# Roots and gates of an attention pair in a PSUM work bank, and the pair's steps at other times in the common order

## The reference

```python
q = _rmsnorm(q, q_rms_w); k = _rmsnorm(k, k_rms_w)
omega_eff = jax.nn.softplus(omega) * slopes
gate = jax.nn.softplus(jnp.einsum('bthd,hd->bht', k, u_n) / math.sqrt(D))
bias = -dist * omega_eff * gate
attn = jax.nn.softmax(q @ k.T / math.sqrt(D) + bias)        # causal
x = _layernorm(x + attn @ v @ Wproj)
h = silu(x @ w1) * (x @ w2); h = gelu(h @ h1); h = gelu(h @ h2)
x = _layernorm(x + h @ w3)
```

## Time and profile before

| | |
|---|---|
| median of 3 runs | 3588.65 us (3587.58 to 3588.75) |
| profiled execution | 3589.89 us, span 3588.1 us |
| granted TensorE clock, mean | 0.959 |
| TensorE, VectorE, ScalarE, GpSimd busy | 90%, 51%, 50%, 42% of the span |
| pairs | 16, each 143 to 144 us |

### The profile page before, as it was taken

How to read it: one execution, slowest core, us unless ns; L and a number is a source line. 1 busy time by engine, 2 the same in 40 slices (tenths; PEclk the granted TensorE clock), 3 DMA queues, 4 the chain that set the end, 5 groups by cost and what they waited for, 6 DMA issues and landing times. The chain is left out here.

```text
span 3588.1 us, 45839 instructions
## 1 busy us (share of the span) xinstructions
PE 3216.2 (90%) x15472; PEld 2476.9 (69%) x15472; DVE 1842.8 (51%) x3921; ACT 1789.9 (50%) x3057; POOL 1513.0 (42%) x1318
## 2 busy tenths in 40 slices
PE   3989989889889898898998988958999999899999
PEld 3756757667567676675665766747877777688887
DVE  7576576665765766657656566614222222133222
ACT  1656656666666666666665666733222232232222
POOL 4565566566655665566655655631111110000000
PEclk8999999999999999999999999979999999999999
DMA  2231322322313223123132231343222331222120
GB/s 71 70 88 25 83 57 54 88 53 59 89 40 91 56 54 88 47 62 91 24 86 56 55 88 36 75 117 97 88 89 85 96 88 65 84 88 71 36 71 18
DMA packets 196538, 249.12 MB, mean 69 GB/s; under 512 B 67280, under 2 KB 95056, under 8 KB 196176
## 3 DMA queue, kind: packets, MB, share of 16 engines
q1 hardware_dynamic: 196304, 246.19, 26.2%
HBM read 84.86 MB, written 43.52 MB: 36 GB/s over the span
## 5 line engine op out<-in xcount | busy, mean ns | idle before, releaser
L366 POOL TENSOR_TENSOR e_lo<-e_all,e_hi 128x512 fp32r<-128x512 f32 (+1 forms) x832 | 1043.9, 1260 | 855.6 <-ACT e_all L606 721.8
L606 ACT ACTIVATE e_all<-ps_s,bias 128x512 f32<-128x512 f32 (+3 forms) x1280 | 781.0, 621 | 213.9 <-PE ps_s L901 143.5
L599 ACT ACTIVATE e_hi<-ps_s,bias 128x512 fp32r<-128x512 f32 (+1 forms) x832 | 558.4, 671 | 300.8 <-PE ps_s L899 178.2
L786 DVE TENSOR_REDUCE maxes<-ps_m 128x1 f32<-128x512 f32 x768 | 520.6, 687 | 356.5 <-PE ps_m L879 347.7
L879 PE MATMUL ps_m<-k_ext,q_max 128*128 128x512 f32 (+3 forms) x1280 | 477.8, 390 | 122.7 <-DVE maxes L786 74.3
L898 PE MATMUL ps_s<-q_twice,k_split 128*128 128x512 f32 (+3 forms) x1280 | 481.0, 376 | 0.7
L899 PE MATMUL ps_s<-q_ext,k_ext 128*128 128x512 f32 (+3 forms) x1280 | 475.7, 372 | 0.0
L932 PE MATMUL ps_v<-e_lo,v_main 128*66 128x512 f32 (+1 forms) x832 | 442.5, 532 | 14.9 <-POOL e_lo L366 14.9
L879 PEld LDWEIGHTS ps_m<-k_ext,q_max 128*128 128x128 f32 x1280 | 244.2, 192 | 302.6 <-DVE maxes L786 138.7
L783 DVE CUSTOM_DVE_ANT_0 ps_m<-ps_m,mask_row 128x128 f32<-128x128 f32 (+3 forms) x512 | 253.0, 497 | 287.2 <-PE ps_m L879 285.4
L916 PE MATMUL ps_v<-e_all,v_full 128*66 128x512 f32 (+2 forms) x896 | 333.3, 454 | 0.0
(11 more groups left out here) (212 smaller groups left out, 6137.8 us busy)
## 6 DMA issues: line engine op xcount, KB each, us to landing
q_twice<-q_max SPq DMA_DIRECT2D x256, 128.0 KB, 2.3
yt<-y_out SPq DMA_DIRECT2D x128, 130.0 KB
k_ext<-kq_hi SPq DMA_DIRECT2D x128, 128.0 KB, 2.3
q_max<-kq_hi SPq DMA_DIRECT2D x128, 128.0 KB, 2.4
k_split<-kq_hi SPq DMA_DIRECT2D x128, 128.0 KB, 2.4
k_split<-kq_lo SPq DMA_DIRECT2D x128, 128.0 KB, 2.4
q_ext<-kq_lo SPq DMA_DIRECT2D x128, 128.0 KB, 2.4
y_in<-yt SPq DMA_DIRECT2D x128, 128.0 KB, 3.1
```

What stands on the lines that cost most here:

```text
L366: on.tensor_tensor(e_lo[:, i % LO_RING, off:QB], e_all[:, u_ % E_RING, off:QB], e_hi[:, i % HI_RING, off:QB].bitcast(F32), ALU.subtract).t ...
L599: nc.scalar.activation(e_hi[:, i % HI_RING, off:QB], ps_s[u_ % 2][:, off:QB], ACT.Exp, bias=by).then_inc(hi_done, 1)
L606: nc.scalar.activation(e_all[:, u_ % E_RING, off:QB], ps_s[u_ % 2][:, off:QB], ACT.Exp, bias=by).then_inc(ex_done, 1)
L786: nc.vector.tensor_reduce(maxes[:, qt, kc:kc + 1], ps_m[m % 2][:, 0:width], AX.X, ALU.max).then_inc(mx_free, 1)
```

## The change

It has three parts. Roots and gates work on tensors of which one is always in PSUM: "root" becomes a user of the work banks, `scratch` cuts its bank into the pieces `rs`, `root_t`, `g` and `c_jc`, the softplus series is shorter by two terms, and the scaled logits and the slope product are made twice, once in each memory. The norms count on a semaphore of their own, `normed`, without waiting for one another, and the first turn waits for it instead of for `gate`. The DMA of the hi half of `k_split` counts on `lo_dup` instead of `hi_dup`. And the table of times is another.

```diff
-        at(H - 3.4 + 0.16 * j, "x in", 1, j)
-        at(H - 3.1 + 0.16 * j, "x", 1, j)
+        at(H - 2.50 + 0.07 * j, "x in", 1, j)
+        at(H - 2.38 + 0.07 * j, "x", 1, j)
...
-            at(t0 - 0.84 + 0.01 * i, "root", p, i)
-        at(t0 - 0.78, "gate a", p)
-        at(t0 - 0.75, "gate exp", p)
+            at(t0 - 1.00 + 0.01 * i, "root", p, i)
+        at(t0 - 0.95, "gate a", p)
+        at(t0 - 0.92, "gate exp", p)
...
-            start, end = (turns[0] + 0.07, t0 + 0.28) if s == 0 else (t0 + 0.29, t0 + 1.29)
+            start, end = (turns[0] + 0.07, t0 + 0.20) if s == 0 else (t0 + 0.24, t0 + 1.08)
...
+        works = [s for s in steps if s[0] in ("project", "turn") or s[0] == "root" and s[2] == 0 or s[0] == "x" and s[1] == 1]
         work_no = {step: i for i, step in enumerate(works)}
-        GATE = 2 + 8 + 14 + 2 + 2 + 1
+        GATE = 3 + 2 * GATE_PARTS
...
-            eng.wait_ge(hi_dup[i % 2], 48 * (i // 2 + 1))
+            eng.wait_ge(hi_dup[i % 2], 32 * (i // 2 + 1))
...
+            if kind == "root":
+                eng.wait_ge(gate, GATE * (a + 1))
+                eng.wait_ge(normed, 8 * (a + 1))
+
+        def scratch(bank):
+
+
+
+            of_root = [bank[:, 4 * TT * i:4 * TT * (i + 1)].rearrange("p (i t) -> p i t", t=TT) for i in range(2)]
+            return (*of_root, bank[:, 8 * TT:20 * TT].rearrange("p (i h t) -> p i h t", h=2, t=TT),
+                    bank[:, 20 * TT:24 * TT].rearrange("p (i h t) -> p i h t", h=2, t=TT))
+
+        def pair_scratch(p):
+            return scratch(work_bank(("root", p, 0)))
...
-                    sp.dma_start(k_split[s][0:D, cols].bitcast(F32), kq_hi[i % 2][0:D, :].bitcast(F32)).then_inc(hi_dup[i % 2], 16)
+                    sp.dma_start(k_split[s][0:D, cols].bitcast(F32), kq_hi[i % 2][0:D, :].bitcast(F32)).then_inc(lo_dup[i % 2], 16)
...
-                e, sm, z, pl, r = (g[:, i, 0:heads, :] for i in (1, 2, 3, 4, 5))
+            def softplus(link, g, heads, part):
+
+                sm, r, s_ps, z, out = (g[:, i, 0:heads, :] for i in (1, 2, 3, 4, 5))
+                x_in, e, s_sb, pl = (t[:, 0:heads, :] for t in (gx, ge, gs, gp_sum))
                 if part == 0:
                     link(nc.vector.tensor_scalar(sm, e, 2.0, None, ALU.add))
                     link(nc.vector.reciprocal(r, sm))
                 if part == 1:
-                    link(nc.vector.tensor_tensor(sm, e, r, ALU.mult))
-                    link(nc.vector.tensor_tensor(z, sm, sm, ALU.mult))
+                    link(nc.vector.tensor_tensor(s_sb, e, r, ALU.mult))
+                    link(nc.vector.tensor_tensor(s_ps, e, r, ALU.mult))
                 if part == 2:
-                    link(nc.vector.tensor_scalar(pl, z, 1.0 / 15, None, ALU.mult))
-                for k in {2: (13,), 3: (11, 9), 4: (7, 5), 5: (3,)}.get(part, ()):
-                    link(nc.vector.scalar_tensor_tensor(pl, pl, 1.0 / k, z, ALU.add, ALU.mult))
+                    link(nc.vector.tensor_tensor(z, s_sb, s_ps, ALU.mult))
+                    link(nc.vector.tensor_scalar(pl, z, ARTANH[5], None, ALU.mult))
+                for k in {3: (4, 3), 4: (2, 1)}.get(part, ()):
+                    link(nc.vector.scalar_tensor_tensor(pl, pl, ARTANH[k], z, ALU.add, ALU.mult))
                 if part == 5:
-                    link(nc.vector.scalar_tensor_tensor(pl, pl, 1.0, sm, ALU.add, ALU.mult))
-                if part == 6:
-                    link(nc.vector.tensor_scalar(r, x_ap, 0.0, None, ALU.max))
-                    link(nc.vector.scalar_tensor_tensor(out_ap, pl, 2.0, r, ALU.mult, ALU.add))
+                    link(nc.vector.scalar_tensor_tensor(z, pl, ARTANH[0], s_ps, ALU.add, ALU.mult))
+                    link(nc.vector.scalar_tensor_tensor(out, x_in, 0.0, z, ALU.max, ALU.add))
...
+                    rs, root_t, _, _ = pair_scratch(p)
                     if i == 0:
                         rooted = [ROOT * p]
                         dve.wait_ge(ss_done, 8 * (p + 1))
+                        work_free(dve, step)
...
-                        rlink(nc.vector.tensor_scalar(root_t[:].bitcast(I32), mean_sq[:].bitcast(I32), 1, None, ALU.logical_shift_right))
-                        rlink(nc.vector.tensor_scalar(rs[:].bitcast(I32), root_t[:].bitcast(I32), -1.0, float(0x5F3759DF), ALU.mult, ALU.add))
+                        rlink(nc.vector.tensor_scalar(root_t.bitcast(I32), mean_sq[:].bitcast(I32), 1, None, ALU.logical_shift_right))
+                        rlink(nc.vector.tensor_scalar(rs.bitcast(I32), root_t.bitcast(I32), -1.0, float(0x5F3759DF), ALU.mult, ALU.add))
                     else:
-                        rlink(nc.vector.tensor_tensor(root_t[:], rs[:], rs[:], ALU.mult))
-                        rlink(nc.vector.scalar_tensor_tensor(root_t[:], root_t[:], -0.5, mean_sq[:], ALU.mult, ALU.mult))
-                        rlink(nc.vector.scalar_tensor_tensor(rs[:], root_t[:], 1.5, rs[:], ALU.add, ALU.mult))
+                        rlink(nc.vector.tensor_tensor(newton[:], mean_sq[:], rs, ALU.mult))
+                        rlink(nc.vector.scalar_tensor_tensor(newton[:], newton[:], -0.5, rs, ALU.mult, ALU.mult))
+                        rlink(nc.vector.scalar_tensor_tensor(rs, newton[:], 1.5, rs, ALU.add, ALU.mult))
...
-                    glink(nc.vector.tensor_tensor(g[:, 6, :, :], logits, rs[:, 2:4, :], ALU.mult))
-                    glink(nc.vector.scalar_tensor_tensor(g[:, 0, :, :], g[:, 6, :, :], -1.0, g[:, 6, :, :], ALU.mult, ALU.min))
+                    rs, _, g, _ = pair_scratch(p)
+                    for x_out in (gx[:], g[:, 0, :, :]):
+                        glink(nc.vector.tensor_tensor(x_out, logits, rs[:, 2:4, :], ALU.mult))
+                    glink(nc.vector.scalar_tensor_tensor(gs[:], gx[:], -1.0, g[:, 0, :, :], ALU.mult, ALU.min))
+                    rs = pair_scratch(p)[0]
                     col, rows = (q_cols(0), q_cols(1), k_cols(0), k_cols(1))[i // 2], slice(i % 2 * HT, (i % 2 + 1) * HT)
-                    glink(nc.vector.tensor_tensor(raw[:, rows, col:col + D], raw[:, rows, col:col + D],
-                                                  rs[:, i // 2, rows].unsqueeze(2).broadcast_to([P, HT, D]), ALU.mult))
+                    nc.vector.tensor_tensor(raw[:, rows, col:col + D], raw[:, rows, col:col + D],
+                                            rs[:, i // 2, rows].unsqueeze(2).broadcast_to([P, HT, D]), ALU.mult).then_inc(normed, 1)
...
-                    if i < SOFTPLUS_PARTS:
-                        softplus(glink, 2, g[:, 6, :, :], g[:, 7, :, :], i)
-                    if i == SOFTPLUS_PARTS:
-                        glink(nc.vector.tensor_tensor(c_jc[:, 0, :, :], g[:, 7, :, :],
-                                                      omega_eff[:, first:first + 2].unsqueeze(2).broadcast_to([P, 2, TT]), ALU.mult))
+                    softplus(glink, g, 2, i)
+                    if i == 6:
+                        for c in (c_all[:], c_jc[:, 0, :, :]):
+                            glink(nc.vector.tensor_tensor(c, g[:, 5, :, :], omega_eff[:, first:first + 2].unsqueeze(2).broadcast_to([P, 2, TT]), ALU.mult))
+                    if i == 7:
                         glink(nc.vector.tensor_tensor(c_jc[:, 1, :, :], c_jc[:, 0, :, :], key_no[:].unsqueeze(1).broadcast_to([P, 2, TT]), ALU.mult))
-                    if i == SOFTPLUS_PARTS + 1:
-                        glink(nc.vector.tensor_copy(bias_in[:, :, 0, :, :], c_jc[:]))
-                        glink(nc.vector.tensor_tensor(bias_in[:, :, 1, :, :], c_jc[:], bias_in[:, :, 0, :, :].bitcast(F32), ALU.subtract))
+                        glink(nc.vector.tensor_copy(bias_in[:, :, 0, :, :], c_jc))
+                    if i == 8:
+                        glink(nc.vector.tensor_tensor(bias_in[:, :, 1, :, :], c_jc, bias_in[:, :, 0, :, :].bitcast(F32), ALU.subtract))
...
-                        pe.wait_ge(gate, GATE * (n // 2 + 1))
+                        pe.wait_ge(normed, 8 * (n // 2 + 1))
```

More of the change, by code:

```diff
@@ L97, in attention_steps @@
         for t in range(TT):
[L98 removed]
+            at(t0 - 1.72 + 0.030 * t, "project", p, t)
         for i in range(4):
[L100 to L103 removed]
+            at(t0 - 1.44 + 0.05 * i, "square", p, i)
+            at(t0 - 1.38 + 0.05 * i, "sum", p, i)
+            at(t0 - 1.22 + 0.04 * i, "square", p, i + 4)
+            at(t0 - 1.16 + 0.04 * i, "sum", p, i + 4)
         for i in range(ROOT_PARTS):
[L105 to L107 removed]
+            at(t0 - 1.00 + 0.01 * i, "root", p, i)
+        at(t0 - 0.95, "gate a", p)
+        at(t0 - 0.92, "gate exp", p)
         for i in range(8):
[L109 removed]
+            at(t0 - 0.95 + 0.025 * i, "norm", p, i)
         for i in range(GATE_PARTS):
[L111 removed]
+            at(t0 - 0.90 + 0.02 * i, "gate b", p, i)
         for s in range(2):
             n = 2 * p + s
[L114 removed]
+            first = t0 - 0.66 if s == 0 else t0 + 0.015
             at(first, "bias", n)
             for i in range(5):
[L117 removed]
```

(33 more changed lines are left out.)

31 lines of the change are left out of this document (14 added, 17 removed).

## The result

The changed kernel takes 3413.16 us (median of 4 runs, 3411.95 to 3416.66), the kernel before 3588.7 beside it: a ratio of 0.9511, 95% interval 0.9494 to 0.9527. The profiled execution has a span of 3414.9 us. All of the gain is in attention: its last value product starts at 2185.60 us instead of 2360.60, 175.0 earlier.

What follows compares the result with a forecast made beforehand. TensorE, busy 90% of the span, was taken as the bound, losing time in attention to waits for the gate chain. Terms of -5.0 us a pair, times 15, with +3.5 once gave -71.5: about 3517 us, range 3450 to 3588.

Steps and rivals of the forecast that it cites:

- turn's wait: TensorE's first turn of a pair: the 6.2 us wait for `bias_out` goes, 1.9 us waiting for the norms is left.
- row of biases: First maximum of a pair: the round trip of `bias_out` through HBM is no longer covered, +1.5 us a pair.
- k_split: Its hi DMA leaves the wait of turns, one issue of 0.57 us less: -0.5 us a pair.
- maxima: TensorE's waits for VectorE's maxima: -0.6 us a pair in the first head, +0.3 in the root chain.
- clock: TensorE's half-clock stretches: shorter waits at the turn and first maximum give -1.4 us a pair, of at most 2.6.
- first pair, once: 30 maxima instead of 23 before the first scores, less later savings and a shorter chain: +3.5 us once.
- The burst of maxima in the root chain: Two gaps of about 2.3 us between maxima instead of one of 3.2: waits of 1.6 + 1.4 us, net +0.3.
- The gate's length: VectorE's chain from the roots' start R: norms end at R + 18.9, gate at R + 20.1, against R + 29.8.
- The first rival: TensorE never meets the chain, PSUM access costs nothing: 3445 to 3470 us, up to 3490 with part of the clock; chance 0.22.
- Slower: Rival: the chain does not get shorter, instructions slow themselves or PSUM access costing 0.2 us; for instance 3650 us; chance 0.12.
- the wait comes back: Rival: the wait returns almost whole, through `e_lo` behind value copies or more maxima waits: 3550 to 3595 us; chance 0.18.
- The case of more waits for maxima: Second cause within the rival of 3550 to 3595 us: more maxima waits and two clock drops a pair, each up to 2 us and more.

## Why the prediction was wrong

The direction and the mechanism at the turn were right, the size was not, and most of the miss is one term. Per pair, forecast and measured:

| term | forecast | measured | from |
|---|---|---|---|
| turn's wait | -6.2 + 1.9 | -6.2 | 93.2 to 0 |
| row of biases, `k_split` | +1.5 - 0.5 | +2.8 | 22.3 to 64.3 |
| maxima | -0.6 + 0.3 | -5.6 | 96.5 to 12.3 |
| clock | -1.4 | -3.3 | TensorE's busy time, 2038.1 to 1988.9 |
| first pair, once | +3.5 | +6.0 | 99.34 to 105.31 |

Measured terms: -12.3 x 15 + 6.0 = -178.5, of -175. The new waits of scores for `e_all`, 3.1 us, had no term and take back most of the rest.

- **Maxima: the step that failed.** The term costed the two places I looked at, the 1.30 and the 2.15 of the earlier trace rows, and put the rest of the 74.3 us in the earlier trace rows (and the 22.2 behind masked maxima) at nothing. The waits at 508.38 (0.99 us), 541.57 (0.84) and 624.67 (0.54) were in the trace. 84 us of them went, where 5 were forecast: 79 of the 104 us by which I was off. Beside the roots they went from 47.4 to 4.7 us, 2.8 less a pair where the sum had 0.3 more, mostly by the memory; elsewhere from 49.1 to 7.6, 2.8 less a pair where it had 0.6, mostly by the table.
- **The burst of maxima in the root chain** was to wait 1.6 + 1.4 us. It waits 0.31 at 445.79: the six small instructions take 1.5 us together, not 2.3, since `mean_sq` was no longer held (0.19 instead of 0.89) and a step costs 0.26 instead of 0.32.
- **The gate's length.** I put the norms' end at R + 18.9; it is R + 16.1: 28 steps at some 0.06 less (1.7), `mean_sq` 0.7 less, eight norms at 0.60 instead of 0.67 (0.6); the list then gives 15.9. TensorE was to be at the turn at R + 17.0; its turn starts at R + 16.1, so it is there by then. Of the turn's 1.9 us some 0.2 are left. The first rival had this, with its cause (a PSUM access that costs nothing), but only 3445 to 3490 us, as it took over the maxima's term.
- **The row of biases.** I took 5.7 us from the gate to the first maximum, from the first pair. Later pairs take 6.7 to 7.9, the one shown 6.9: `yt`, `recip_sums` and the first turn's two DMAs are in SyncE's queue ahead of the row. With the gate ending 0.9 us behind the turn instead of 1.2, the wait is 3.1 instead of 1.7.
- **Clock.** One stretch at half clock is left of two, as the sum had it in kind. The 0.55 of the earlier trace rows is not behind the 2.15 us of the earlier trace rows at 472.86, but behind an equal wait of the next pair, at 617.33; behind the one at 472.86 the clock is 0.66 for 3 us. That a stretch is left in 12 of 15 pairs goes with the wait for the row: in the version with the turn at t0 - 0.62 it is left in three. That version is 21 us faster, while its listed waits at maxima are only 6 us less (71.0 for 76.6); TensorE's busy time in attention is 17 us less.
- **k_split, first pair**: 0.57 for 0.5, and 6.0 for 3.5. In the first pair the maxima start 3.8 us earlier (76.72 for 80.52), but it is 28.6 us from there to the first scores instead of 18.8. Seven more maxima were to be 5.7 of that; the wait for `q_twice`, 2.2, had no term.
- **Slower, or the wait comes back**: nothing of either. `e_lo` keeps its 1 us wait a pair, 15.5 us for 14.9. The case of more waits for maxima did not come either: there are fewer.

## What to carry to other kernels

A term for each row of the waits view, with its whole total, comes before any term for a place looked at: what has no term is forecast as unchanged. If one engine's short instructions are held up by another engine, their delay is paid not only by who waits for the chain but by all that stands behind it in the same queue, and taking it away pays in both. Before a step is moved, ask which chains end at its consumer and which DMA issues it passes in the queue; of five later turns one helped; behind it the queue and the second chain took over.
